# Attention with a routed mixture of experts on one core: the indirect row writes are dealt out two to a group, and two weight splits move into the first groups

## What is computed

```python
h = rmsnorm(xn) * norm_scale                      # per token
q, k, v = h @ wq, h @ wk, h @ wv                  # 16 heads of 64
attn = softmax(q * 64**-0.5 @ k.T) @ v  ->  @ w_out + b_out
logits = silu(xn @ rw1 + rb1) @ rw2 + rb2         # 8 experts
top-2 of logits, softmax over the two -> weights
experts = sum_e weight_e * ((silu(xn @ w1[e] + b1[e])) @ w2[e] + b2[e])
```

## Time and profile before

| | |
|---|---|
| median of three timed runs | 2058.65 us |
| profiled execution, its own time | 2047.12 us |
| its span, first to last instruction | 2045.3 us |
| mean granted TensorE clock, share of full | 0.989 |
| busy share PE, DVE, ACT, POOL | 96%, 79%, 74%, 45% |
| indirect writes of routed rows (L666) | 128 |

### The profile page before, as it was taken

One profiled execution on the slowest core, in us unless ns is written; L12 is line 12 of the kernel. 1 busy time (PEld: TensorE's weight loads), 2 busy tenths in 40 slices (PEclk: granted clock), 3 DMA queues, 4 the chain that ended last, 5 costly groups with the idle time before them and its releaser, 6 DMA issues.

```text
span 2045.3 us, 45195 instructions
## 1 busy us (share of the span) xinstructions
PE 1955.3 (96%) x16646; PEld 1257.6 (61%) x16646; DVE 1624.6 (79%) x2798; ACT 1506.4 (74%) x3572; POOL 930.1 (45%) x794
## 2 busy tenths in 40 slices
PE   7999999989999999989999999999999999999998
PEld 5656555556555555556666666666666666666664
DVE  7878788888888887877777777777777877777786
ACT  5767676767666666656878788888787888887865
POOL 4435364654444444310364554644645546446430
PEclk9999999999999999999999999999999999999999
DMA  2113222321111111113243333433433434334220
GB/s 84 36 56 105 80 93 75 107 77 40 40 38 38 38 43 33 34 48 93 71 79 92 80 79 89 85 85 79 84 86 79 88 81 89 88 79 84 58 37 28
DMA packets 132761, 142.22 MB, mean 70 GB/s; under 512 B 25486, under 2 KB 99086, under 8 KB 132494
## 3 DMA queue, kind: packets, MB, share of 16 engines
q1 hardware_dynamic: 101374, 118.34, 18.4%
q0 software_dynamic: 31168, 20.99, 9.0%
HBM read 102.92 MB, written 38.72 MB: 69 GB/s over the span
## 4 chain that ended last, share of the span: by engine, by line
PE 72%; DVE 11%; ACT 9%; issue 4%; POOL 1%; DMA 1%; another core or an unknown queue 0%; SPq 0%; DVEq 0%; ACTq 0%; POOLq 0%
PE pair L455 20%; PE pair L396 15%; PE pair L426 10%; PE pair L240 6%; PE pair L242 4%; PE pair L241 4%; DVE NM L405 4%; ACT PR L411 3%; PE pair L501 2%; PE pair L503 2%; DVE PT L441 2%; PE pair L788 1%; PE pair L790 1%; PE pair L789 1%; ACT ZT L763 1%
## 5 line engine op out<-in xcount | busy, mean ns | idle before, releaser
L411 ACT ACTIVATE PR<-pair,NM 128x512 f32<-128x512 f32 x1024 | 710.9, 717 | 30.6 <-DVE NM L405 28.0
L405 DVE TENSOR_REDUCE NM<-pair 128x2 f32<-128x1024 f32 x512 | 611.5, 1210 | 44.8 <-PE pair L396 34.8
L438 ACT COPY PT<-pair 128x512 f32<-128x512 f32 x512 | 277.2, 599 | 396.4 <-PE pair L426 395.8
L396 PE MATMUL pair<-KS,QS 64*128 64x512 f32 x3072 | 489.2, 422 | 25.9 <-ACT HS L560 10.3
L455 PE MATMUL pair<-PT,V 128*64 128x512 f32 x2048 | 474.6, 606 | 2.1 <-ACT PR L411 2.0
L426 PEld LDWEIGHTS pair<-idn,PR 64*128 64x128 f32 x8192 | 336.9, 139 | 103.9 <-ACT HS L560 22.8
L780 POOL TENSOR_TENSOR HH<-ZZ,HH 128x512 fp32r<-128x512 f32 x156 | 201.4, 1355 | 413.6 <-ACT HH L777 413.6
L396 PEld LDWEIGHTS pair<-KS,QS 64*128 64x128 f32 x3072 | 256.0, 187 | 194.2 <-issue 141.5
L426 PE MATMUL pair<-idn,PR 64*128 64x64 f32 x8192 | 343.5, 223 | 21.4 <-ACT HS L560 16.4
L441 DVE COPY PT<-pair 128x512 f32<-128x512 f32 x512 | 327.1, 680 | 8.0 <-remote 5.1
L455 PEld LDWEIGHTS pair<-PT,V 128*64 128x64 f32 x2048 | 137.1, 138 | 263.0 <-issue 248.5
(11 more groups left out here) (168 smaller groups left out, 2831.6 us busy)
## 6 DMA issues: line engine op xcount, KB each, us to landing
E<-w_tab SPq DMA_DIRECT2D x78, 512.0 KB
RB<-l_rows SPq DMA_DIRECT2D x127, 256.0 KB
XG<-slots SPq DMA_DIRECT2D x39, 264.0 KB
w_tab<-SPL SPq DMA_DIRECT2D x16, 512.0 KB
l_rows<-RT SPq DMA_DIRECT2D x508, 1.0 KB
xin<-in_x SPq DMA_DIRECT2D x16, 256.0 KB, 7.7
XQ<-in_x SPq DMA_DIRECT2D x16, 256.0 KB, 7.4
RAW<-in_w SPq DMA_DIRECT2D x16, 256.0 KB
```

Source lines behind the costliest of these rows:

```text
L396: m = e.matmul(bank[bk + j], a[half[j], cols], c[half[j], :], start=(k == 0), stop=(k == 2))
L405: add("dve", lambda e: e.tensor_reduce(NM[:, 2 * t:2 * t + 2], both[:], AX.X, ALU.max, negate=True), needs=[("S", n, t), *([("exp", n - 1, ...
L411: add("act", lambda e: e.activation(PR[:, k, :], bank[bk], ACT.Exp, bias=NM[:, k:k + 1], accum_out=RS[:, n % 2, j, t:t + 1]), needs=[("max ...
L438: add("act", lambda e, r=r: e.copy(dst[r], src[r]), needs=[("T", n, t), *old], name=("PT", n, t, r), place=f"turn{t % 2}")
```

## The change

Four edits:

1. `scatter` writes two per group in h = 2, 3, 4 and 5, where it wrote three, three and two in h = 2, 3 and 4.
2. Each write also waits for one row maximum of the same group: the first of the two for that of t = 0, the second for that of t = 1.
3. `routed_rows(r + 1)` is called in h = 5 where it was called in h = 4.
4. The splits of the second half of wk and of wq move from the start into the groups 0 and 1.

```diff
-        def scatter(r, part):
-            for k, t in list(itertools.product(range(2), range(QT)))[part]:
+        def scatter(r, part, behind):
+            for (k, t), start in zip(list(itertools.product(range(2), range(QT)))[part], behind):
                 add("pool", lambda e, k=k, t=t: e.indirect_dma_start(
...
-                    needs=[("gate", r, 24), ("tok", r), ("xr", r, 1)], name=("sc", r), step=16, sem=f"sc_{r % 2}")
+                    needs=[("gate", r, 24), ("tok", r), ("xr", r, 1), start], name=("sc", r), step=16, sem=f"sc_{r % 2}")
...
         split_weights("wv", wv_s, WV, [0])
-        split_weights("wk", wk_s, WK, [1], on="dve")
         split_weights("wv", wv_s, WV, [1])
-        split_weights("wq", wq_s, WQ, [1], DH ** -0.5, on="dve")
         split_weights("r1", r1_s, R1, [0])
...
         def starting(G):
+            if G == 0:
+                split_weights("wk", wk_s, WK, [1], on="dve")
+            if G == 1:
+                split_weights("wq", wq_s, WQ, [1], DH ** -0.5, on="dve")
...
-                if 2 <= h <= 4:
-                    scatter(r - 1, slice(3 * h - 6, 3 * h - 3))
+                if 2 <= h <= 5:
+                    scatter(r - 1, slice(2 * h - 4, 2 * h - 2), [("max", G // 2, 2 * (G % 2) + t) for t in range(2)])
...
-                if h == 4:
+                if h == 5:
                     routed_rows(r + 1)
```

## The result

| | before | after |
|---|---|---|
| median of 20 timed runs each, same chip | 2057.98 us | 2066.24 us |
| lowest and highest | 2053.0 to 2061.8 | 2058.4 to 2069.49 |
| profiled execution, its own time | 2047.12 us | 2069.13 us |
| its span | 2045.3 us | 2067.3 us |
| mean granted TensorE clock in it | 0.989 | 0.979 |

The ratio is 1.0039, with a 95% interval of 1.003 to 1.0049: slower, by 8.3 us in the medians. The forecast was 2055.8 us. So the two traces differ by 22.0 us of span where the medians differ by 8.3. Much of that gap is the clock. (1 - granted clock) times the time is what the lower clock takes. Over the timed runs it is 38.8 us for after.

A forecast was written before the change was run, and what follows sets the result against it. PE was taken as the bound, its idle time the stake: -14.0 (A) - 7.8 (B) - 1.8 (C) + 19.2 + 1.5 (D) = -2.9 us, so 2055.8 us from 2058.65, range 2036 to 2077.

The forecast's parts named there:

- What bounds the kernel: Whole kernel: PE is busy 96% of the span; its idle time, mostly in the routing rounds, can be won.
- Term A: Rounds 1 to 15: spreading the writes removes two thirds of 21.3 us of PE stops, 14 us gained.
- term B: Round 16: eight writes become four pairs, removing the 5.9 us stop and slow clock, 7.8 us gained.
- the gate gains nothing: Rival on the writes: late handoffs are not their doing, or cost the same anywhere; 2077.5 us, chance 0.10.
- Term C: Start: moved weight splits bring the first maximum forward by 3.0 us, costing 1.2 later; net gain 1.8 us.
- Term D: Before L340: late rows cost 19.2 us in rounds 3, 5 and 7, and 1.5 us in the others.
- L309's wait for the landing was 1.89 us here, so it starts at 438.2: Round 7: landing time read before the change, putting the rows at 440.3, 4.5 us late for PE.
- at the middle this is on the edge: Rounds 1, 9, 11 and 13: rows at 539.2 to 542.7 against 540.50 in group 68; 1.5 us for all.
- second rival: Before L340: landings of 5.1 us during SP's block load make rows late in seven rounds; 45 us, 2080, chance 0.14.
- The sum: Whole kernel: gains and price together give -2.9 us, from 2058.65 to 2055.8 us, no visible change.

The follow-up runs named there:

- e9_three_rows_h4: Kernel before the change plus paired, gated writes, the start edit and a third XR buffer, rows left in h = 4: 2026.6 us, ratio 0.9866.
- e7_burst8: Kernel before the change with all eight writes of a round in a row in h = 2: 2105.26 us, ratio 1.0265.
- e13_rb_split: Changed kernel with the RB broadcast issued as two DMAs of 64 partitions instead of one: 2045.95 us, ratio 0.9943.
- e15_three_rb_split: e9_three_rows_h4 with the RB broadcast issued as two DMAs of 64 partitions: 2024.59 us, ratio 0.9856.
- e12_load_later: Changed kernel with the call for the next block's XQ load moved to h = 6: 2067.47 us, ratio 1.0066.
- e6_after_again: Changed kernel with all four edits, unchanged, run again on chip 10: 2068.84 us, ratio 1.0084.
- e2_no_start: Changed kernel without the moved wk and wq splits at the start, chip 2: 2061.9 us, ratio 1.0172.
- e5_before_again: Kernel before the change, unchanged, run again on chip 10: 2053.48 us, ratio 1.0009.
- e1_start_only: Kernel before the change with only the wk and wq splits moved into groups 0 and 1, chip 2: 2021.32 us, ratio 0.9984.
- e4_split_last: Changed kernel with the expert weights' split called behind the route part of its group, chip 2: 2030.08 us, ratio 1.0023.

## Why the prediction was wrong, step by step

**What bounds the kernel** was right: PE, and its stops in the routing part.

**Term A and term B were right** in mechanism and nearly in size: -21.8 together. Stops beside writes fell from 27.4 to 9.4 us in the traces: 5.9 of the 18.0 are round 16's (term B), and 12.1 are term A's, 14 forecast. On chip 10 it is 27.3 to 7.8. With the price taken away (e9_three_rows_h4, chip 8) the whole gain was 28.6 us; less 2.5 for the start, as measured on chip 5, it is 26 us, some 4 more than forecast, with the third buffer's own part in it, which wasn't separated. 7 us of that are the clock (0.9898 against 0.9863 as a mean over the timed runs there), of which the forecast had 1.9. The rival "the gate gains nothing" is out where before takes 2053 to 2058 us: moving the same eight writes took the stops from 54.9 us (e7_burst8) through 27.3 to 7.8. By which path POOL's indirect DMAs hold ACT's copies, through ports or otherwise, no run shows. On chip 2 that rival held nearly: there was little to gain. I had taken the late handoffs for a property of the kernel alone.

**Term C was right:** 2.5 and 3.1 us in two comparisons, 1.8 forecast, and the first maximum came 2.9 us earlier, 3.0 forecast.

**Term D failed**, at the step "L309's wait for the landing was 1.89 us here, so it starts at 438.2" and at "at the middle this is on the edge". I took the landing of round 7 from before, where the broadcast came only behind the last write. SP's timeline of before has it at 414.65, 11.6 us ahead of the write of the earlier trace rows at 426.26, and again at 429.10. The third row is the broadcast 1.0 us ahead of the last two writes (478.88 and 480.22) whose landing took the 5.11 us of the earlier trace rows. The load of XQ stands behind it there as well, at 478.99, so this trace alone doesn't say which of the two it was.

```profile
414.65 0.52 SPq L493 DMA_DIRECT2D RB<-l_rows  x1
...
429.10 0.52 SPq L493 DMA_DIRECT2D RB<-l_rows  x1
...
477.85 0.50 SPq L493 DMA_DIRECT2D RB<-l_rows  x1
```

In h = 5 the broadcast comes ahead of the last two writes. The landings were 5.44, 3.25 and 5.53 in the three bad rounds, and 4.6 to 4.9 in rounds 1, 9, 11 and 13. The rest of the step held for rounds 3, 5 and 7. e13_rb_split shows it: with landings of 2.33, 1.59 and 2.98 us in rounds 3, 5 and 7 L340 waited in exactly the three rounds forecast, for 4.30, 4.75 and 4.97 us where 4.5 was forecast, and nowhere else. Its price against e15_three_rb_split in the same comparison is 21.4 us (14.0 of stops, and 7.0 more lost to the clock over the timed runs), and term D was 20.7. With the landing as it was, the price is 40.9 us (e12_load_later against e9_three_rows_h4, one comparison; in the seven rounds e12 is after unchanged). On chip 2 the buffer alone takes 32 us away, with 6.9 us of waits left. In e12's trace the stops before L340 are 30.5 us, but PE's idle time is only 24.4 us above e9's, since other stops shrink; over the timed runs the clock takes 18.9 us more (39.7 against 20.8).

So the second rival is what happened, "the rows are late in seven rounds". It was priced at 45 us against the 40.9, with its point of decision at a landing of some 3 us; the landings went past it. Its reason missed the main cause: I blamed SP's load of the next block. The load is on its way in these rounds in e13_rb_split too, and with the broadcast split the landings are 1.6 to 3.0 us. The 5.11 us of the earlier trace rows and the mean of 3.0 in the earlier trace rows stood in the trace, and I gave the rival 0.14, because the gated writes leave as that load begins. I had not looked which transfers stood ahead of the long landing and not ahead of the short one, nor on how many engines they run.

**The sum.** With D at 40.9, A and B at -26 and C at -2.5 it comes to +12.4, which is by construction what e12_load_later measured against before on chip 8 (+12.3). Measured for the changed kernel itself: +8.3 on the first chip, +16.0 on chip 10 (e6_after_again). So the forecast missed by one term, D, at twice its size. That the total was off by 11 us (+8.3 against -2.9) and not by 20 is in part luck, since A and B came out larger. On chip 2 after itself wasn't run; e2_no_start, which lacks only the start edit, is 37.5 us slower than before there.

**Not settled:** why the handoffs beside writes are late on chips 5, 8 and 10 and in the first comparison, and hardly on chip 2. The order on POOL and the write's 0.96 us are the same there. It isn't the clock either: before loses 27.0 us to it on chip 2 and 28.1 on chip 8, over the timed runs.

## What to carry to other kernels

Before a write is moved to just ahead of something that waits for its landing, look up what SP issues in the few us before it, and on how many DMA engines each of these transfers runs: one that runs on 2 of 16 held the indirect writes behind it for 1.7 to 3.1 us in the seven rounds here, and splitting it cost nothing that could be measured. Before an instruction is called moved, look in the trace where it left: a DMA whose call comes a group later can leave the in-order queue at the same time. A duration of a landing belongs to the place where it was read, and doesn't move along with the instruction. Where a wait exists only because a buffer is reused, a third buffer settles most of it: with it, and with the rows back in h = 4, a change that was 0.4 to 0.8% slower became one that is 1.3% faster (on another chip).

## What the runs showed of the hardware

- The same kernel takes 2024 us on chip 2 and 2053 to 2058 on three others and in the first comparison. What differs in the traces is PE's idle time: 90.8 us in the whole span of e5_before_again on chip 10, 63.5 in e1_start_only on chip 2 (some 3 us of it the start edit's), most of the difference beside POOL's indirect writes (27.3 us in 28 stops, and 4.1 in 5). The size of a gain or loss from moving them depends on the chip: edits 1 to 3 cost 1.7% on chip 2, and all four 0.4 and 0.8% in the first comparison and on chip 10.
- An indirect write of 128 rows lands 1.54 us after POOL is done with it at the quickest (read at the start of L309, which waits for it), and up to 5.5 us after it in after (6.2 in e4_split_last), where the broadcast on two engines is ahead of it.
- A broadcast of 256 KB that runs on 2 of the 16 DMA engines takes 5.8 us for its packets (106.44 to 112.24 in after), and two of 128 KB on all of them 1.7 (106.07 to 107.78 in e13_rb_split).
- The stop of 7.40 us in round 3 brought the lower of TensorE's two clocks with it: from 223 to 234 the granted clock was 0.56 on the mean. Over the timed runs on chip 10 the mean clock is 0.986 for before and 0.981 for after.
